# Transposes and a loss product get slots of their own between the scores of an eight-batch attention kernel

## The reference

```python
q = _split_heads(q_in @ Wq.T)                       # 16 heads of 16 dimensions
k = _split_heads(mem @ Wk.T)
v = _split_heads(mem @ Wv.T)
scores = jnp.einsum('bhqd,bhkd->bhqk', q, k) / jnp.sqrt(jnp.float32(D_HEAD))
attn = jax.nn.softmax(jnp.where(mem_mask, scores, -jnp.inf), axis=-1)
out = jnp.einsum('bhqk,bhkd->bhqd', attn, v)        # then @ Wo.T, add x, layernorm

base = jnp.einsum('btd,de->bte', x, W_base) + b_base
h = jax.nn.relu(jnp.einsum('btd,ndh->nbth', x, W_enc) + b_enc[:, None, None, :])
recon = jnp.einsum('nbth,nhd->nbtd', h, W_dec) + b_dec[:, None, None, :]
losses = jnp.mean((recon - x[None]) ** 2, axis=(2, 3))
top1 = jnp.argmin(losses, axis=0)                   # one of 8 adapters for each batch element
mid = jax.nn.relu(jnp.einsum('btd,bdr->btr', x, Wd) + bd[:, None, :])
adapter_out = jnp.einsum('btr,brd->btd', mid, Wu) + bu[:, None, :]
```

## Time and profile before

| | |
|---|---|
| median of 3 runs | 1649.25 us (1646.03 to 1655.02) |
| profiled execution | 1650.58 us |
| its span, first to last instruction | 1648.8 us |
| mean granted TensorE clock | 0.989 |
| TensorE matmul busy | 1586.7 us, 96% |
| VectorE busy | 1238.2 us, 75% |
| ScalarE busy | 1053.2 us, 64% |
| GpSimd busy | 161.2 us, 10% |
| chain that ended last, by engine | PE 85%, DVE 7%, ACT 3%, issue 3% |

### The profile page before, as it was taken

The page is one execution under the profiler, slowest core; times in us unless marked ns, Lnnn a source line. Parts: engine busy times, 40 slices in busy tenths (PEclk is TensorE's granted clock), DMA queues, the critical chain, the costliest instruction groups (busy, mean ns, idle before and its releaser), DMA issues.

```text
span 1648.8 us, 25559 instructions
## 1 busy us (share of the span) xinstructions
PE 1586.7 (96%) x9632; PEld 588.7 (36%) x9632; DVE 1238.2 (75%) x1790; ACT 1053.2 (64%) x1998; POOL 161.2 (10%) x151
## 2 busy tenths in 40 slices
PE   6779999999999999999999999999999999999997
PEld 5442323332333333332333323433333323332233
DVE  5788777877788777887888777887778777887522
ACT  2227776676666666676666766676666776666661
POOL 7311000100011000100001000110001000000000
PEclk8899999999999999999999999999999999999999
DMA  5655071623517071442707163361707234150010
GB/s 156 116 143 101 25 138 41 101 69 86 96 40 127 28 131 40 90 93 62 116 22 134 32 113 69 69 112 52 121 12 122 61 52 77 50 78 5 11 33 16
DMA packets 118663, 125.22 MB, mean 76 GB/s; under 512 B 35186, under 2 KB 100339, under 8 KB 118540
## 3 DMA queue, kind: packets, MB, share of 16 engines
q1 hardware_dynamic: 117724, 123.06, 38.3%
q10 hardware_dynamic: 816, 0.53, 0.1%
HBM read 84.18 MB, written 35.03 MB: 72 GB/s over the span
## 4 chain that ended last, share of the span: by engine, by line
PE 85%; DVE 7%; ACT 3%; issue 3%; DMA 1%; SPq 0%; POOL 0%; POOLq 0%; DVEq 0%; ACTq 0%
PE banks L1122 23%; PE values L1141 23%; PE banks L1082 12%; PE work L1012 5%; PE work L998 5%; PE work L957 4%; DVE xneg_max_pieces L1439 4%; PE work L1019 3%; PE work L1025 3%; ACT xprobs L1260 3%; PE work L1004 2%; PE work L1028 1%; PE work L942 1%; PE work L1037 1%; DMA max_dram<-xneg_max_rows 1%
## 5 line engine op out<-in xcount | busy, mean ns | idle before, releaser
L1260 ACT ACTIVATE xprobs<-banks 128x512 f32<-128x512 f32 x1664 | 900.5, 595 | 408.3 <-PE banks L1122 405.0
L1439 DVE TENSOR_REDUCE xneg_max_pieces<-banks 128x2 f32<-128x1024 f32 x768 | 909.0, 1219 | 258.4 <-PE banks L1082 257.2
L1122 PE MATMUL banks<-xq_stacks,xk_stacks 99*128 99x512 bf16 (+1 forms) x1664 | 517.7, 385 | 9.9 <-ACT xprobs L1260 3.0
L1141 PE MATMUL values<-xprobs,xv_rows 128*17 128x512 f32 x3328 | 437.9, 598 | 1.3 <-ACT xprobs L1260 1.3
L1122 PEld LDWEIGHTS banks<-xq_stacks,xk_stacks 99*128 99x128 bf16 (+1 forms) x1664 | 127.4, 97 | 398.8 <-ACT xprobs L1260 273.2
L1082 PE MATMUL banks<-xk_stacks,xq_stacks 49*128 49x512 bf16 (+1 forms) x2048 | 250.3, 335 | 14.2 <-DVE xneg_max_pieces L1439 12.3
L1082 PEld LDWEIGHTS banks<-xk_stacks,xq_stacks 49*128 49x128 bf16 x2048 | 57.2, 94 | 327.6 <-DVE xneg_max_pieces L1439 212.9
L1510 POOL TENSOR_TENSOR xk_parts<-xk_rest,xk_parts 128x401 bf16<-128x401 f32 (+1 forms) x64 | 59.0, 923 | 660.5 <-ACT xk_parts L1239 660.5
L1141 PEld LDWEIGHTS values<-xprobs,xv_rows 128*17 128x17 f32 x3328 | 55.1, 95 | 122.9 <-issue 117.6
L1505 POOL TENSOR_TENSOR xrstd<-xrstd,mhalf 128x4 f32<-128x4 f32 x23 | 23.2, 1011 | 652.4 <-DVE xrstd L1314 652.4
L1012 PEld LDWEIGHTS work<-xvT,ctxT_a 128*128 128x128 f32 (+1 forms) x416 | 54.3, 192 | 13.6 <-issue 3.9
(11 more groups left out here) (295 smaller groups left out, 1007.3 us busy)
## 6 DMA issues: line engine op xcount, KB each, us to landing
xk_stacks<-key_parts_dram SPq DMA_DIRECT2D x186, 200.1 KB, 13.0
key_parts_dram<-xk_parts SPq DMA_DIRECT2D x144, 100.0 KB, 2.2
xq_stacks<-parts_dram SPq DMA_DIRECT2D x186, 64.0 KB, 8.8
ctxT_a<-in_ctxT SPq DMA_DIRECT2D x4, 1601.0 KB, 7.5
ctxT_b<-in_ctxT SPq DMA_DIRECT2D x4, 1601.0 KB, 7.5
parts_dram<-xq_parts SPq DMA_DIRECT2D x45, 128.0 KB, 2.0
key_parts_dram<-xk_parts SPq DMA_DIRECT2D x48, 100.2 KB, 5.2
xa<-in_x SPq DMA_DIRECT2D x8, 512.0 KB, 16.3
```

The source lines that it names most:

```text
L1122: pe.matmul(at, kst[0:ROWS[par], k, h2, par, t * P:(t + 1) * P], qst[0:ROWS[par], k, h2, par, :], start=True, stop=True).then_inc(made, 1)
L1141: last = pe.matmul(av[32 * j:32 * j + HD + 1, :], vals[:, k, t, gr * GH + j, :], probs[:, sl % 2, j, :], start=t == 0, stop=t == XKT - 1)
L1260: nc.scalar.activation(probs[:, sl % 2, j, :], score_bank(n)[0], ACT.Exp).then_inc(exped, 1)
L1439: nc.vector.tensor_reduce(nmp[:, of % 2, :, j2, q, piece], pairs[n % MRING][:, :, :], AX.X, ALU.max, negate=True).then_inc(on["mxr"], 1)
```

## The change

`x1T`, `x2T` and `loss` leave `IN_BETWEEN` and become jobs with a slot of their own in `SLOT_END`; `v 3` moves from slot 18 to 19. Five jobs give up a slot for them: `xo 0`, `xo 1`, `qproj 0` and `mid` go from two slots to one, `gram 2` from three to two. In a slot whose job is one of the three short ones, the max tiles now stand last, behind the scores of heads 2 and 3 and behind the job, as they did before in slots with no job. VectorE scales the last heads' output ahead of two normalisation steps in slot 5, and the steps for `x2` come a slot earlier.

```diff
--- before.py
+++ after.py
@@ -829,18 +829,17 @@
         on = dict(front)
 
         NOW, NEXT, PREV = 0, 1, -1
-        IN_BETWEEN = {
-            8: ("x1T", 0, NEXT), 11: ("x1T", 1, NEXT), 14: ("x2T", 0, PREV), 16: ("x2T", 1, PREV), 18: ("v", 3, NOW),
-            35: ("loss", 0, PREV),
-        }
+        SHORT = ("x1T", "x2T", "loss")
+        IN_BETWEEN = {19: ("v", 3, NOW)}
         SLOT_END = [
             (("kproj", 0, NEXT), 1), (("kproj", 1, NEXT), 1), (("v", 0, NOW), 2), (("v", 1, NOW), 2),
-            (("xo", 0, PREV), 2), (("xo", 1, PREV), 2), (("kproj", 2, NEXT), 1), (("kproj", 3, NEXT), 1),
-            (("qproj", 0, NEXT), 2), (("v", 2, NOW), 2), (("enc", 0, PREV), 2), (("gram", 0, PREV), 2),
+            (("xo", 0, PREV), 1), (("xo", 1, PREV), 1), (("x1T", 0, NEXT), 1), (("x1T", 1, NEXT), 1),
+            (("kproj", 2, NEXT), 1), (("kproj", 3, NEXT), 1), (("qproj", 0, NEXT), 1), (("x2T", 0, PREV), 1),
+            (("x2T", 1, PREV), 1), (("v", 2, NOW), 2), (("enc", 0, PREV), 2), (("gram", 0, PREV), 2),
             (("enc", 1, PREV), 2), (("kproj", 4, NEXT), 1), (("gram", 1, PREV), 2), (("enc", 2, PREV), 2),
-            (("gram", 2, PREV), 3), (("enc", 3, PREV), 2), (("gram", 3, PREV), 2), (("kproj", 5, NEXT), 1),
-            (("kproj", 6, NEXT), 1), (("kproj", 7, NEXT), 1), (("v", 4, NEXT), 2), (("v", 5, NEXT), 2),
-            (("mid", 0, PREV), 2), (("y", 0, PREV), 2), (("y", 1, PREV), 2), (("v", 6, NEXT), 2),
+            (("gram", 2, PREV), 2), (("enc", 3, PREV), 2), (("gram", 3, PREV), 2), (("loss", 0, PREV), 1),
+            (("kproj", 5, NEXT), 1), (("kproj", 6, NEXT), 1), (("kproj", 7, NEXT), 1), (("v", 4, NEXT), 2),
+            (("v", 5, NEXT), 2), (("mid", 0, PREV), 1), (("y", 0, PREV), 2), (("y", 1, PREV), 2), (("v", 6, NEXT), 2),
             (("qproj", 1, NEXT), 2), (("v", 7, NEXT), 1),
         ]
         AT_END = [(job, part, parts) for job, parts in SLOT_END for part in range(parts)]
@@ -862,10 +861,10 @@
             27: [("invert", "o", 1, NOW)], 32: [("scale", "o", 1, NOW)],
             40: [("invert", "o", 2, NOW)], 44: [("scale", "o", 2, NOW)],
             2: norm_steps("stats", "x1", 0, 2, NEXT), 3: norm_steps("stats", "x1", 2, 4, NEXT),
-            5: [*norm_steps("apply", "x1", 0, 2, NEXT), ("scale", "o", 3, PREV)],
-            6: norm_steps("apply", "x1", 2, 4, NEXT), 8: norm_steps("stats", "x2", 0, 2, PREV),
-            9: norm_steps("stats", "x2", 2, 4, PREV), 10: [("aggr", "x2", 0, PREV)],
-            11: norm_steps("apply", "x2", 0, 2, PREV), 12: norm_steps("apply", "x2", 2, 4, PREV),
+            5: [("scale", "o", 3, PREV), *norm_steps("apply", "x1", 0, 2, NEXT)],
+            6: norm_steps("apply", "x1", 2, 4, NEXT), 7: norm_steps("stats", "x2", 0, 2, PREV),
+            8: norm_steps("stats", "x2", 2, 4, PREV), 9: [("aggr", "x2", 0, PREV)],
+            10: norm_steps("apply", "x2", 0, 2, PREV), 11: norm_steps("apply", "x2", 2, 4, PREV),
             35: choose_steps(0, 4), 36: choose_steps(4, 8), 37: choose_steps(8, CHOOSE_STEPS),
             45: norm_steps("stats", "y", 0, 2, PREV), 47: norm_steps("stats", "y", 2, 4, PREV),
             48: [("aggr", "y", 0, PREV)], 49: norm_steps("apply", "y", 0, 2, PREV),
@@ -1159,14 +1158,15 @@
                 pe_values(sl - 1)
             if short:
                 pe_job(MAIN, short)
-            if job:
+            tiles_last = job is None or job[0] in SHORT
+            if not tiles_last:
                 pe_max_tiles(m, t)
             if not final:
                 pe_scores(m, t, 2)
                 pe_scores(m, t, 3)
             if job:
                 pe_job(MAIN, job, part, parts)
-            else:
+            if tiles_last:
                 pe_max_tiles(m, t)
```

## The result

The changed kernel takes 1655.95 us (median of nine runs, 1651.21 to 1661.02), the kernel before 1649.25 (nine runs beside them, 1646.03 to 1655.02). The ratio is 1.0037, with a 95% interval of 1.0024 to 1.005, so 4.0 to 8.3 us slower. Ratios and intervals here are estimated from the single runs and differ a little from the quotient of two medians. One run of e1 and one of e2, 1.6% and 9% longer at a lower mean clock (0.94 and 0.85), count in their medians and not in their ratios. The change is within the 0.5% that the prediction called no change; it gave 1655.3. The interval is narrower than the prediction thought possible, and it doesn't contain 1: the kernel is slower, by about 0.4%.

The account below looks back on a forecast made before the run. TensorE was taken to set the time. Savings of 1.55 us against costs of 2.63 lengthen a middle batch by 1.08, six by 6.5; less 0.5 in the last, +6.0 gives 1655.3 us, range 1646 to 1663.

Parts of the forecast that it names:

- Seam at slot 10, 1.17; at slot 15, 0.67; at slot 35, 0.14: Where tiles-last meets tiles-first, TensorE waits for VectorE in the two-tile ring: 1.17, 0.67 and 0.14 us added per middle batch.
- rival 1: VectorE's free 39 us a batch absorb the waits at slots 10, 15 and 35: 1643.4 us, chance 0.10.
- Scale first, 0.48: Slot 6: scaling ahead of normalisation removes TensorE's wait before `xo`, 0.48 us saved a middle batch.
- slot 11, 0.30; slots 8 and 14, 0.14: `x1T` and `x2T` behind second scores no longer wait for bank `work`: 0.30 and 0.14 us saved a middle batch.
- `mid`, 0.23: `mid` done whole instead of in two halves saves 0.23 us a middle batch.
- half jobs, 0.40: Ten half jobs become whole, saving 0.02 to 0.05 us each, 0.40 a middle batch.
- ScalarE's pile at slots 13 and 14, 0.65: Slots 13 and 14: ScalarE's copies crowd between exponentials and delay TensorE, 0.65 us added a middle batch.
- Order scores, transposes, tiles: New TensorE order in the five short-job slots: taken as 0, within -0.1 and +0.1 us a slot.
- Last batch -0.5: Last batch: an existing wait moves to a slot without the turning into rows, -0.5 us, bounds 1.5 either side.
- First batch 0, within 1.5: First batch: new waits at slots 10 and 15, an existing one milder; 0 us, bounds -1.5 and +1.5.
- Rival 2: Slot 39's first scores wait for late rows of maxima, 1.2 us a batch more: 1662.4 us, chance 0.20.
- Rival 3: Waits only change places, with slots 10, 15 and 35 at half price: 1648.5 us, chance 0.20.

Follow-up runs that it names:

- e1: Changed kernel with max tiles ahead of the second scores again in all slots that have a job; 1653.07 us, ratio to before 0.9999.
- e2: Changed kernel with SyncE's write and read back of slot 39's maxima ahead of the parts of `kproj 5`; 1655.47 us, ratio to before 1.0017.
- e10: Kernel before with max tiles last only in slot 9 of each batch, nothing else moved; single run, 1662.64 us.
- e11: Changed kernel with VectorE turning maxima into rows behind the slot's second reduction instead of between the two; 1650.1 us, ratio to before 0.9991.
- e3: Kernel before with only VectorE's scaling of the last heads put ahead of two normalisation steps in slot 5; 1650.94 us, ratio 0.9991.
- e8: Kernel before, unchanged, run once more for its first batch; single run, 1653.55 us.
- e7: Kernel before with scale first, `xo` and `mid` whole, statistics earlier, `x1T` and `x2T` in neighbouring slots but ahead of the tiles; 1647.22 us, ratio 0.9971.
- e4: Changed kernel with max tiles last in every slot and VectorE's copy of a finished job ahead of the slot's maxima; 1690.23 us, ratio to before 1.0231.
- e12: e7 with the load of x issued nine slots later; 1644.32 us, ratio to the kernel before 0.9959.

## Why the prediction was right, and where it was not

The sign and the time came out (+6.0 forecast, +6.7 between medians, +6.1 by the ratio). By its own steps:

- **Seam at slot 10, 1.17; at slot 15, 0.67; at slot 35, 0.14.** Measured 1.17, 0.65 to 0.67, and 0.15. Reading them off places of the same pattern held to a few hundredths. e10 makes the cause shown: one seam in the old kernel gives the same idle 0.98. Placing the statistics of slot 9 where they do no harm was right too (1.7 to 2.5 us into the slot, the first reduction at 2.9). e11 then splits the cost of slot 10 between the ring and the turning into rows.
- **VectorE's free 21%** did not absorb anything (rival 1). e1, e10 and e11 agree in that with the trace. The Trainium skill, Perfetto Trace Analysis, "Identifying the Most-Contended Engine", calls VectorE's occupancy a fair measure of how close that engine is to its roofline. It doesn't say that nothing waits for an engine with time to spare; that was the prediction's step, and here it fails (VectorE 79% busy, 0.98 us of idle TensorE in slot 10). e11 shows one thing that decides: what stands between the two reductions.
- **Scale first, 0.48; slot 11, 0.30; slots 8 and 14, 0.14; `mid`, 0.23; half jobs, 0.40.** TensorE has no idle row at any of these places, `mid` takes the 1.86 that was counted for a whole one, and the half `xo` of slot 6, which had taken 0.94 and not 0.86, gives 0.08 more. The half jobs gave less, 0.30: the step from first scores to values fell from 0.58 to 0.53 in six slots, not in ten. And the 0.48 was argued as if it stood by itself; e3 shows that it doesn't: alone the edit is worth 0.11.
- **ScalarE's pile at slots 13 and 14, 0.65.** 0.28 in slot 13 (3.32 less 3.04 free) and 0.30 in slot 14, 0.58. For slot 13 0.27 was forecast; of the 0.38 for slot 14 (0.26, and 0.12 for the copy of `x2T 0`) 0.30 came.
- **Order scores, transposes, tiles: 0 taken, within 0.1 a slot.** This term was mis-sized: four sets of transposes take 0.53 to 0.54 behind scores where they took 0.59, 0.22 in all, and `loss` 0.66 instead of 0.77, so the five short slots are 0.33 cheaper together. With 0.07 of the pile and 0.08 of the half `xo`, less the 0.10 that the half jobs didn't give, that is 0.38 of the 0.40 by which a middle batch came out better than forecast (+0.68, not +1.08).
- **Last batch -0.5.** Measured -0.51.
- **First batch 0, within 1.5.** The two profiled executions differ by +3.64, outside the bounds. But e8 shows the kernel before at 178.99 too, and e11, with the changed order, has 175.96. Over the twelve profiles first batches lie at 174.4 to 176.4 or at 178.7 to 179.3, with both orders in both groups. The change does make the rows leave 3.6 us later there (`kproj 5` has moved from slot 34 to 35, and the rows stand behind its parts), and it may make the long wait more frequent; with one profile of each kernel this isn't settled.

So the nearly exact total is partly luck. The steady terms give 6 x 0.68 (3.8 in the profiles, where the fifth batch of before is 189.30, and 189.32 in e8) less 0.5, about +3.3. e2, whose middle batches are the changed kernel's, measures +2.8 (ratio 1.0017) beside its own runs of before; the first pair gave +6.1 by the ratio, with 4.0 as the low end of its interval. In the profiles the rest lies in the first batch, which varies by 5 us over the twelve (174.4 to 179.3), and in the front, whose length varies as much (117.8 to 122.6) though no edit is aimed at it. The kernel before itself had medians of 1652.01, 1652.56 and 1651.24 in the three groups, above the 1649.25 that the prediction started from.

**Rival 2** had the mechanism (the first scores of slot 39 wait for their rows) but not the place: its own objection, that the trip is long only while other traffic is under way, was right for the middle batches, where the trip fell from 3.9 to 6.6 us to 2.0 to 3.2. **Rival 3** was wrong for the seams; they came at full price.

## What to carry to other kernels

When two orders of the same steps meet, price the seam: count the producer's tiles that fall together, and the consumer's time for the ring's depth, with all that the consumer does between. A place in the profile where the same pattern already occurs gave the price here to a few hundredths of a microsecond. And a stall removed alone may return a slot or two later (0.48 became 0.11), so that edits which remove stalls are best tried together with those that give their producer room, as in e7.

## What the runs showed of the hardware

- **A short idle cost more than itself.** TensorE had been idle for 2.75 us until 257.87, and at 259.1 its granted clock fell. Stretches around it in the changed kernel (columns as in the earlier trace rows):

```profile
250.00:255.00 5.00, 5.00 (x30) 2.36 (x28) 4.09 (x5) 3.95 (x8) 1.75 (x2) 1.00 0.65 138
255.00:260.00 5.00, 2.25 (x16) 0.38 (x14) 0.86 (x1) 1.51 (x4) 0.00 (x0) 0.91 0.33 105
260.00:266.00 6.00, 6.00 (x37) 3.22 (x34) 4.28 (x5) 3.16 (x7) 0.00 (x0) 0.79 0.17 41
```

  From 259.1 to 262.5 it was at the lower level, 1.2 GHz; the tiles took 1.04 instead of 0.61, and the slot 4.96 instead of 3.41. After 2.00 us in e8 the same happened (a slot of 4.98); after 1.37 us in e11 and 0.89 in the kernel before, a slot of 3.40 followed at 2.4 GHz. So 1.55 us come on top of the wait. That parts the first batches into two groups: the five profiles from 178.7 up (after, e1, e2, e3, e8) have waits of 2.00 to 3.03 us and the lower clock behind them, and six others have waits of 0 to 1.37 us and no lower clock. Only e4, whose slots are ordered otherwise, has a long wait (2.86) and the lower clock at 176.12.
- **What a matmul costs depends on its neighbours.** Four transposes take 0.54 behind scores and 0.58 to 0.59 behind values; half a `v` takes 0.89 up to scores and 0.99 up to tiles, 0.10 more. Why, no run here shows.
- **A small transfer took longer in busier company.** From the issue of the rows' write to that of the read back it is 2.1 us where the DMA engines are 0.24 busy meanwhile (changed kernel, third batch), 5.2 where they are 0.55 busy (before), and 9.1 where they are 0.79 busy (before, first batch); sending it earlier (e2) only lengthened it. Moving the load of x away (e12) shortened it in the middle batches and left 7.9 us in the first.
- **Most middle batches repeat** to about 0.01 us within an execution and between executions of a kernel (189.01, 189.02), so terms of 0.05 us can be read there that ratios of the whole, with intervals 0.25% wide, never show. Not all do: the fifth batch of the kernel before is 189.30, and 189.32 in e8, so "nearly to the nanosecond" in the section on the profile before holds for five of the six, and e3 has one of 189.57 and one of 189.21.
